# A transformer block on one core: half batch 0's second norm is turned by TensorE in fp32, the filling rows lie on four partitions, and every engine's order is new

## Chip, cores and metric

The kernel runs on one core of a Trainium2 chip. The metric is the device time of one execution in microseconds (us). The profile is of one execution; its span goes from the first instruction to the last.

## The reference

x has 4 batches of 512 rows of 256 numbers, the context 4 x 512 x 512 (256 numbers of keys, 256 of values), the mask 4 x 512.

```python
x = x + tanh(g_xattn[0]) * xattn(ctx, layernorm(x), mask, b)
x = x + tanh(g_ffn[0])   * ffn(layernorm(x), w_gate, w_up, w_down)

# xattn: 8 heads of depth 32
logits  = einsum('bhqd,bhkd->bhqk', Q * depth**-0.5, K) + b[0] - 1e30 * (1 - mask)
out     = einsum('bhqk,bhkd->bhqd', softmax(logits), V)
# ffn: 256 -> 768 -> 256, integer weights times 1/127
h       = silu(x @ wg.T) * (x @ wu.T);  y = h @ wd.T
```

The mask is 1 only at keys at the end of a batch's 512, and every key where it is 0 gets -1e30. So the main path of the kernel takes the last 128 keys alone; a flag computed on the way chooses a general path after it, which these inputs do not take.

## The kernel before

The work is cut into 8 half batches (256 rows each, numbered r = 0 to 7; batch b = r // 2). Every engine has a list of steps written out by hand as short codes in `ORDER` (lines 163 to 205); `step_of` turns a code into a step, and each engine runs its list strictly in order, with waits on semaphores for what other engines make. The codes that matter here:

- `sa`/`sb` statistics of the first/second layer norm (VectorE lines 968 to 977, then GpSimd's power at 658), `na`/`nb` the norm itself in fp32 (VectorE 992 or GpSimd 669, 681), `ha`/`hb` its fp16 high part (ScalarE 745), `la`/`lb` its low part, norm minus high (GpSimd 688), `du` a doubled copy of the query's parts (VectorE 1002).
- `qs` queries turned by TensorE and copied by ScalarE (batch 0), `qn` queries turned by a DMA on SP's queue (batches 1 to 3).
- `kp` the key's high part (VectorE 1048), with its low part on GpSimd (693); `kr` that of batch 0 on VectorE (1040); `ks` keys turned by TensorE and copied out of PSUM by VectorE or ScalarE (1085, 772). From batch 1 on the keys are turned against a matrix `fillers` and not against the identity, so that masked keys are replaced by a mean of the others. `fr` (fill_row, VectorE 1013 to 1017) makes the rows for it from the mask, `ft` (fill_t, TensorE 1284 and 1286, VectorE 1022) the matrix. `br` is the mask row of batch 0 (1007).
- `rm` row maxima of the logits (TensorE 1333, VectorE 1122), `mx` their transpose, `sc` logits and exponential (TensorE 1378 and 1380, ScalarE 821), `ws` weighting of the values and sums (TensorE 1399 and 1404, ScalarE 832 and 834), `at` transpose of the result in fp32 (TensorE 1450), scaling (VectorE 1153 and 1155) and the residual add that makes the new x (GpSimd 698).
- `nn` the second norm turned by a DMA transpose of its high and low parts on SP's queue (582), for halves 0 to 6; `nt` the same by TensorE in fp16, for half 7. `wc`/`wn` cast and DMA transpose of the three weights.
- `hi` six hidden units per half: 8 matmuls (1503), tanh (ScalarE 869), `pr` two VectorE products (1166, 1177), `hs` split of h into fp16 high (ScalarE 878) and low (GpSimd 705), `do` the down projection (TensorE 1529), `fi` finish: residual and store.
- `wu` warm-ups: 3 or 4 matmuls of 512 columns whose result nobody reads (1241), 25 in all; 14 more run at the start.
- `sq`, `ck`, `fs` checks for the flag.

TensorE's results go to eight PSUM banks; the working steps take two of them in turn, and four before the first hidden unit. A step waits until the last user of its bank is emptied (`open_work`). A hidden unit waits for the product of the one two before it.

`norm32` has four slots, and a norm that takes a slot again waits until the low part of the norm that had it is made (`wait_norm_used`).

Of the kernel before, what the change touches and what calls it, by code (L numbers as in the profile page):

```python
# [148 lines left out]
def norm1_on_pool(step):  # L149
# [20 lines left out]
        at2.0 at2.1 sc3.2 hi0.3 ks2.0 hi0.4 rm4.0 ks2.1 hi0.5 do0.0 do0.1 sc3.3 rm4.1 do0.2 rm4.2 hi1.0 hi1.1 do0.3  # L170
        rm4.3 hi1.2 ws3 hi1.3 mx4 hi1.4 at3.0 sc4.0 hi1.5 rm5.0 at3.1 sc4.1 do0.4 do0.5 ks3.0 sc4.2 hi2.0 sc4.3 rm5.1
        hi2.1 ws4 hi2.2 rm5.2 hi2.3 at4.0 ks3.1 do1.0 hi2.4 rm5.3 at4.1 do1.1 do1.2 mx5 do1.3 hi2.5 rm6.0 hi3.0 do1.4
        rm6.1 sc5.0 do1.5 hi3.1 sc5.1 hi3.2 sc5.2 rm7.0 hi3.3 sc5.3 rm6.2 hi3.4 ws5 rm6.3 do2.0 do2.1 at5.0 mx6 hi3.5
        at5.1 do2.2 sc6.0 hi4.0 rm7.1 sc6.1 rm7.2 sc6.2 hi4.1 sc6.3 rm7.3 hi4.2 ws6 mx7 do2.3 hi4.3 do2.4 sc7.0 hi4.4
# [1396 lines left out]
```

## Time and profile before

| what | us |
|---|---|
| median of 3 runs | 137.76 |
| lowest, highest | 137.49, 138.76 |
| profiled execution | 137.66 |
| its span | 135.8 |
| TensorE matmuls busy | 125.0 (92%) |
| VectorE busy | 104.6 (77%) |
| GpSimd busy | 94.0 (69%) |
| ScalarE busy | 91.5 (67%) |

The granted TensorE clock is 0.994 of full speed over the span. The busy share of TensorE counts each matmul to its modelled end, so in a dense stream matmuls overlap and the share is 100%; how far apart they start tells the pace. In the lists PE is TensorE, DVE VectorE, ACT ScalarE, POOL GpSimd, SPq the DMA queue of SP.

### The profile page before, as it was taken

To read this page: it belongs to the slowest core of one execution; us is meant where nothing else is said; L and a number is where in the kernel's file an instruction comes from. 1 tells how busy PE (TensorE), PEld (TensorE's weight loads), DVE (VectorE), ACT (ScalarE), POOL (GpSimd) and SP (SyncE) were. 2 spreads that over 40 slices of the span, in tenths; PEclk is the share of its full clock that TensorE was granted. 3 is DMA by queue.
4 is the path that set the end of the run, shared out by engine and by line. 5 is a ranking of instruction groups with operands and counts; after the bars stand their busy time and mean duration, and the time that the engine had idled before them with its cause. 6 is when DMAs were issued, how large, how long until landed. Compare 5 with 4: busy or idle time off the path is not lost.

```text
span 135.8 us, 3716 instructions
## 1 busy us (share of the span) xinstructions
PE 125.0 (92%) x1276; PEld 97.6 (72%) x1276; DVE 104.6 (77%) x296; ACT 91.5 (67%) x206; POOL 94.0 (69%) x146
## 2 busy tenths in 40 slices
PE   7759799997999997999999999999999999999980
PEld 2245564764868895798799877977986987988860
DVE  1799999999655999599797895796677898678441
ACT  2429997783999867778597896876773644774610
POOL 7464769397999999667956663717866798662920
PEclk9999999999999999999999999999999999999997
DMA  3949999694495404430089702100320080201023
GB/s 127 285 127 369 370 352 155 119 186 89 83 157 116 77 5 76 97 58 7 0 165 234 69 2 57 25 0 0 75 84 0 5 233 1 77 7 47 30 86 92
DMA packets 32050, 14.08 MB, mean 104 GB/s; under 512 B 25605, under 2 KB 31257, under 8 KB 32025
## 3 DMA queue, kind: packets, MB, share of 16 engines
q1 hardware_dynamic: 31984, 13.77, 43.7%
q8 instruction: 12, 0.20, 0.6%
q14 instruction: 14, 0.11, 0.3%
q10 hardware_dynamic: 40, 0.01, 0.0%
HBM read 5.52 MB, written 2.10 MB: 56 GB/s over the span
## 4 chain that ended last, share of the span: by engine, by line
PE 60%; DVE 16%; POOL 9%; DMA 4%; issue 4%; SPq 3%; ACT 2%; DVEq 0%; ACTq 0%; POOLq 0%
PE ps L1503 26%; PE ps L1529 11%; DMA gates<-in_L_xattn_b_dram 4%; PE ps L1399 4%; PE ps L1404 4%; PE ps L1378 4%; PE ps L1380 4%; DVE max_cols L1122 4%; PE ps L1450 3%; PE ps L1333 2%; DVE stats L968 2%; POOL x_sb L698 2%; POOL h L705 2%; DVE gated L1166 2%; POOL q_parts L688 2%
## 5 line engine op out<-in xcount | busy, mean ns | idle before, releaser
L1503 PE MATMUL ps<-n_t,w_gu_t 128*128 128x256 f16 x384 | 49.0, 273 | 0.9 <-DVE h L1177 0.7
L1503 PEld LDWEIGHTS ps<-n_t,w_gu_t 128*128 128x128 f16 x384 | 36.4, 98 | 7.1 <-DVE h L1177 2.1
L705 POOL TENSOR_TENSOR h<-h 128x256 f16<-128x256 f32 x48 | 31.5, 674 | 7.5 <-ACT h L878 7.5
L1166 DVE SCALAR_TENSOR_TENSOR gated<-tanh_h,ps 128x256 f32<-128x256 f32 x48 | 19.9, 415 | 12.3 <-ACT tanh_h L869 11.9
L869 ACT ACTIVATE tanh_h<-ps 128x256 f32<-128x256 f32 x48 | 18.3, 382 | 13.1 <-PE ps L1503 10.9
L1529 PE MATMUL ps<-w_d_t,h 128*128 128x256 f16 x192 | 25.7, 273 | 0.0
L821 ACT ACTIVATE probs<-ps,exp_bias 128x512 f32<-128x512 f32 x32 | 21.6, 686 | 4.3 <-PE ps L1380 4.1
L1122 DVE TENSOR_REDUCE max_cols<-ps 128x4 f16<-128x512 f32 x32 | 21.4, 684 | 2.9 <-PE ps L1333 2.6
L1177 DVE SCALAR_TENSOR_TENSOR h<-ps,gated 128x256 f32<-128x256 f32 x48 | 20.4, 425 | 2.4 <-POOL h L705 0.8
L878 ACT ACTIVATE h<-h 128x256 f16<-128x256 f32 x48 | 18.5, 412 | 4.6 <-DVE h L1177 4.3
L1529 PEld LDWEIGHTS ps<-w_d_t,h 128*128 128x128 f16 x192 | 18.4, 98 | 2.1
L698 POOL TENSOR_TENSOR x_sb<-x_sb,attn 128x256 f32<-128x256 f32 x16 | 11.6, 733 | 8.7 <-DVE attn L1155 8.5
L1378 PE MATMUL ps<-q_stacks,k_stacks 128*128 128x256 f16 x64 | 15.6, 273 | 0.4 <-ACT max_rows L810 0.3
L1380 PE MATMUL ps<-max_rows,kv_rest 128*128 128x256 f16 x64 | 15.5, 273 | 0.0
L968 DVE BATCH_NORM_STATS2 stats<-x_sb 128x6 f32<-128x256 f32 x32 | 11.6, 413 | 4.6 <-DMA x_sb<-in_x_dram 2.5
L658 POOL TENSOR_TENSOR rstd<-var_eps,neg_half 128x2 f32<-128x2 f32 (+1 forms) x13 | 10.5, 806 | 6.7 <-DVE var_eps L977 6.6
L688 POOL TENSOR_TENSOR norm<-norm 128x512 f16<-128x512 f32 x8 | 9.3, 1160 | 6.4 <-ACT norm L745 6.2
L688 POOL TENSOR_TENSOR q_parts<-norm,q_parts 128x512 f16<-128x512 f32 x8 | 9.4, 1180 | 5.8 <-ACT q_parts L745 5.8
L1333 PE MATMUL ps<-k_stacks,q_stacks 128*128 128x128 f16 x128 | 12.1, 219 | 0.0
L1333 PEld LDWEIGHTS ps<-k_stacks,q_stacks 128*128 128x128 f16 x128 | 9.1, 98 | 2.3 <-issue 0.6
L681 POOL TENSOR_SCALAR norm<-x_sb,neg_mean,rstd 128x256 f32<-128x256 f32 x16 | 9.1, 579 | 0.5
L832 ACT ACTIVATE o_sb<-ps 128x512 f32<-128x512 f32 x8 | 4.8, 596 | 6.3 <-PE ps L1404 6.2
(102 smaller groups left out, 180.4 us busy)
## 6 DMA issues: line engine op xcount, KB each, us to landing
x_sb<-in_x_dram SPq DMA_DIRECT2D x8, 256.0 KB, 6.0
out_dram<-x_sb SPq DMA_DIRECT2D x7, 256.0 KB, 2.6
kv<-in_ctx_dram SPq DMA_DIRECT2D x4, 256.0 KB, 6.1
w_raw<-in_L_ffn_w_gate_dram SPq DMA_DIRECT2D x1, 768.0 KB, 7.8
w_raw<-in_L_ffn_w_up_dram SPq DMA_DIRECT2D x1, 768.0 KB, 9.6
w_raw<-in_L_ffn_w_down_dram SPq DMA_DIRECT2D x1, 768.0 KB, 8.4
out_dram<-x_sb SPq DMA_DIRECT2D x2, 128.0 KB, 2.3
q_stacks<-q_parts SPq DMA_TRANSPOSE x12, 3.3
```

Of the source, the lines that this page charges most:

```text
L688: pool.tensor_tensor(low, full, high, ALU.subtract).then_inc(norm_low, 1)
L705: pool.tensor_tensor(h16[:, r % 2, m, 1, :], h32[:, n % NHB, :], h16[:, r % 2, m, 0, :], ALU.subtract).then_inc(h_low, 1)
L821: act.activation(probs[:, j % NPB, :], bank32(SCORES[j % 2]), ACT.Exp, bias=key_bias[:, n:n + 1] if is_wide else exp_bias[:, b:b + 1], sca ...
L878: act.activation(h16[:, r % 2, m, 0, :], h32[:, n % NHB, :], ACT.Copy).then_inc(h_high, 1)
L1122: dve.tensor_reduce(dst, bank32(plan.bank(step)).rearrange("p (h k) -> p h k", h=HG), AX.X, ALU.max, negate=not is_wide).then_inc(emptied_ ...
L1166: mine(dve.scalar_tensor_tensor(out=gated[:, n % 2, :], in0=tanh_h[:, n % 2, :], scalar=1.0, in1=got[:, 0:SH], op0=ALU.add, op1=ALU.mult))
L1177: dve.scalar_tensor_tensor(out=dst, in0=got[:, SH:2 * SH], scalar=0.5 * W_SCALE * W_SCALE * H_SHRINK, in1=gated[:, n % 2, :], op0=ALU.mult ...
L1333: ins = pe.matmul(bank32(n)[:, j * P:(j + 1) * P], q_stacks[:, b, qt, h, :], k_stacks[:, b, h, :], start=(j == 0), stop=(b >= FILL_FROM an ...
L1378: pe.matmul(dst, k_stacks[:, b, h, :], q_stacks[:, b, 2 * half:2 * half + 2, h, :], start=(i == 0), stop=False, skip_group_check=True)
L1380: ins = pe.matmul(dst, (max_sel if is_wide else max_sel16)[:, h, :], (max_rows if is_wide else max_rows16)[:, rows, :], start=False, stop= ...
L1503: ins = pe.matmul(dst, lhs, rhs, start=(w == 0 and (k, l) == terms[0]), stop=(k, l) == terms[-1], skip_group_check=True)
L1529: ins = pe.matmul(dst, lhs, rhs, start=(m == 0 and l == 0 and (t == 0 or r == R - 1)), stop=(m == MT - 1), skip_group_check=True)
```

## The change

Three changes of steps, and new orders for all five engines.

1. Half 0's second norm is no longer split by ScalarE and GpSimd and turned by a DMA (`hb0`, `lb0`, `nn0`). TensorE turns it in fp32 (four transposes) into one PSUM bank; ScalarE copies that to fp16 as the high part; VectorE subtracts this from PSUM for the low part (`nc0`, n_copies).
2. The last mask row of each batch is loaded to a partition of its own, four in all, so that fill_row's three operations are 4x128 in place of 1x384. On TensorE each of three matmuls picks one of the four rows with a selector matrix.
3. The constant tile `ones16` is gone.

```diff
-N_BY_DMA = (0, 1, 2, 3, 4, 5, 6)
+N_BY_DMA = (1, 2, 3, 4, 5, 6)
+N_BY_COPIES = (0,)
...
     "sp": """
-        qn2 wn1 qn3 wn0 nn0 wn2 qn4 nn1 qn5 nn2 nn3 qn6 fi0 qn7 nn4 nn5 fi1 nn6 fi2 fi3 fi4 fi5 fi6 fi7""",
+        qn2 qn3 wn1 wn0 qn4 wn2 qn5 nn1 qn6 qn7 fi0 nn2 fi1 nn3 nn4 fi2 nn5 nn6 fi3 fi4 fi5 fi6 fi7""",
     "pe": """
-        ks0 mt qs0.0 wu5 wu0 qs0.1 rm0.0 rm0.1 wu7 rm0.2 qs1.0 rm0.3 mx0 rm1.0 qs1.1 rm1.1 wu3 sc0.0 sc0.1 rm1.2 sc0.2
-        ft sc0.3 rm1.3 wu6 ws0 ks1.0 mx1 wu2 at0.0 ks1.1 at0.1 sc1.0 rm2.0 rm2.1 wu4 rm2.2 sc1.1 rm2.3 sc1.2 sc1.3
-        rm3.0 rm3.1 mx2 ws1 rm3.2 sc2.0 rm3.3 sc2.1 at1.0 sc2.2 at1.1 mx3 sc2.3 wu1 sc3.0 sc3.1 hi0.0 ws2 hi0.1 hi0.2
...
+        wu0 mt wu6 ks0 qs0.0 wu5 qs0.1 wu1 rm0.0 wu4 ft rm0.1 qs1.0 rm0.2 rm0.3 qs1.1 rm1.0 rm1.1 mx0 wu7 rm1.2 rm1.3
+        sc0.0 sc0.1 wu3 ks2.0 sc0.2 ks1.0 sc0.3 ks1.1 wu2 mx1 ws0 sc1.0 rm2.0 rm2.1 ks2.1 at0.0 sc1.1 ks3.0 rm2.2
+        at0.1 sc1.2 rm2.3 sc1.3 rm3.0 rm3.1 mx2 ws1 sc2.0 rm3.2 sc2.1 rm3.3 at1.0 nc0 sc2.2 rm4.0 mx3 sc2.3 at1.1
+        hi0.0 sc3.0 hi0.1 sc3.1 rm4.1 ws2 sc3.2 rm4.2 hi0.2 rm4.3 hi0.3 do0.0 at2.0 hi0.4 mx4 do0.1 rm5.0 sc3.3 at2.1
+        hi0.5 sc4.0 do0.2 ks3.1 rm5.1 sc4.1 hi1.0 rm5.2 ws3 rm5.3 sc4.2 do0.3 hi1.1 mx5 sc4.3 at3.0 hi1.2 at3.1 sc5.0
+        rm6.0 do0.4 hi1.3 do0.5 rm6.1 sc5.1 hi1.4 ws4 rm6.2 hi1.5 sc5.2 at4.0 do1.0 rm6.3 hi2.0 do1.1 rm7.0 hi2.1 mx6
...
     "dve": """
-        sa0 kp0 br na0 mc kr0 sa1 du0 ks0 mt na1 sa2 rm0.0 du1 eb rm0.1 rm0.2 rm0.3 fr rm1.0 kp1 du2 sa4 rm1.1 rm1.2
-        ft rm1.3 sa6 ks1.0 du3 at0.0 at0.1 rm2.0 rm2.1 rm2.2 sb0 rm2.3 rm3.0 kp2 kp3 rm3.1 du4 rm3.2 rm3.3 at1.0 at1.1
...
+        sa0 kp0 fr na0 kr0 mc sa1 br du0 mt na1 ks0 sa2 rm0.0 du1 kp1 ft rm0.1 eb rm0.2 rm0.3 rm1.0 kp2 rm1.1 rm1.2
+        sa4 du2 rm1.3 ks1.0 kp3 du3 sa6 rm2.0 rm2.1 at0.0 rm2.2 at0.1 rm2.3 du4 sb0 rm3.0 rm3.1 rm3.2 rm3.3 at1.0 nc0
+        rm4.0 at1.1 pr0.0 sb1 ys du5 rm4.1 pr0.1 rm4.2 pr0.2 rm4.3 at2.0 pr0.3 rm5.0 pr0.4 at2.1 pr0.5 rm5.1 rm5.2 du6
+        pr1.0 sb2 rm5.3 pr1.1 at3.0 at3.1 du7 rm6.0 pr1.2 fi0 rm6.1 pr1.3 pr1.4 sb3 rm6.2 at4.0 pr1.5 rm6.3 rm7.0
...
     "act": """
-        ha0 qs0.0 eb ha1 qs0.1 wc0 qs1.0 ha2 wc1 mx0 qs1.1 sc0.0 sc0.1 ha3 sc0.2 sc0.3 wc2 ws0 ha4 mx1 ks1.1 sc1.0 sq0
-        sc1.1 sc1.2 sc1.3 hb0 mx2 ws1 sc2.0 sc2.1 sc2.2 mx3 sc2.3 sq1 ha5 sc3.0 sq2 hi0.0 sc3.1 ws2 hi0.1 ha6 hb1
...
+        ha0 qs0.0 ha1 eb qs0.1 wc0 qs1.0 ha2 qs1.1 mx0 wc1 ha3 sc0.0 sc0.1 ks2.0 sc0.2 sc0.3 ks1.1 mx1 ha4 ws0 sc1.0
+        ks2.1 ha5 sc1.1 ks3.0 sc1.2 sc1.3 wc2 mx2 sq0 ws1 sc2.0 sc2.1 nc0 mx3 sc2.2 hi0.0 sc2.3 hs0.0 sc3.0 hi0.1 sq1
...
     "pool": """
-        sa0 la0 sa1 la1 sa2 na2 la2 na3 la3 sa4 kp1 na4 at0.0 at0.1 sa6 la4 sb0 nb0 lb0 kp2 na5 at1.0 at1.1 na6 la5
...
+        sa0 la0 sa1 la1 sa2 na2 kp1 na3 la2 kp2 la3 sa4 na4 kp3 na5 sa6 la4 at0.0 at0.1 sb0 nb0 at1.0 la5 at1.1 sb1
...
-        mask_row = sb("mask_row", [1, B, P], I32)
+        mask_row = sb("mask_row", [B, P], I32)
...
-        fill_row = sb("fill_row", [P, NF, P], F16)
+        fill_row = sb("fill_row", [P, P], F16)
...
+        def n_copies_out(step):
+            got = bank32(plan.bank(step)).rearrange("p (t k s) -> p t k s", t=2, k=KD)
+            return [n_t16[:, step[1] % 2, :, l * KD:(l + 1) * KD, :] for l in range(2)], got
...
 (ScalarE)
-            act.dma_start(mask_row[:, :, :], mask[:, LAST * P:SK].unsqueeze(0)).then_inc(mask_row_loaded, 16)
+            act.dma_start(mask_row[:, :], mask[:, LAST * P:SK]).then_inc(mask_row_loaded, 16)
...
+                        act.wait_ge(work_filled, plan.filled(step))
+                        parts, full = n_copies_out(step)
+                        act.activation(parts[0], full, ACT.Copy).then_inc(n_high, 1)
...
 (VectorE, fill_row)
-                        mine(dve.tensor_reduce(neg_count[:, :], mask_row[:, FILL_FROM:B, :], AX.X, ALU.add, negate=True))
+                        mine(dve.tensor_reduce(neg_count[:, :], mask_row[:, :], AX.X, ALU.add, negate=True))
                         wait_mine()
                         mine(dve.reciprocal(share[:, :], neg_count[:, :]))
                         wait_mine()
-                        dve.scalar_tensor_tensor(out=fill_row[0:1, :, :], in0=mask_row[:, FILL_FROM:B, :], scalar=1.0,
-                                                 in1=share[:, :].unsqueeze(2).to_broadcast((1, NF, P)),
-                                                 op0=ALU.subtract, op1=ALU.mult).then_inc(fill_row_ready, 1)
+                        dve.tensor_scalar(fill_row[0:B, :], mask_row[:, :], 1.0, share[:, 0:1], ALU.subtract, ALU.mult
+                                          ).then_inc(fill_row_ready, 1)
...
 (VectorE, n_copies)
+                        dve.wait_ge(n_high, plan.nth[step] + 1)
+                        parts, full = n_copies_out(step)
+                        dve.tensor_tensor(parts[1], full, parts[0], ALU.subtract).then_inc(emptied_by["dve"], 1)
...
 (TensorE, fill_t)
-                        pe.matmul(bank32(n)[:, 0:NF * P], ones16[:, :], fill_row[:, :, :], start=False, stop=True,
-                                  skip_group_check=True).then_inc(work_filled, 1)
+                        for i in range(NF):
+                            ins = pe.matmul(bank32(n)[:, i * P:(i + 1) * P], max_sel16[:, FILL_FROM + i, :], fill_row[:, :],
+                                            start=False, stop=(i == NF - 1), skip_group_check=True)
+                        ins.then_inc(work_filled, 1)
...
 (TensorE, n_copies)
+                        pe.wait_ge(normed2, plan.nth["norm2", r] + 1)
+                        for t in range(2):
+                            for k in range(KD):
+                                ins = pe.transpose(bank32(n)[:, (KD * t + k) * P:(KD * t + k + 1) * P],
+                                                   norm32[:, ln_slot("norm2", 2, r), t, k * P:(k + 1) * P], ident32[:, :])
+                        ins.then_inc(work_filled, 1)
...
+                            elif not is_wide and r in N_BY_COPIES:
+                                pe.wait_ge(*plan.emptied(("n_copies", r)))
```

## Rows read from the trace of the kernel before

**Rows 1.** Busy us (instructions) per engine by stretch of the span; then clock, DMA, GB/s.

```profile
...
8.90:38.04 29.14, 26.38 (x279) 18.00 (x280) 26.68 (x81) 23.73 (x41) 21.58 (x26) 1.00 0.83 214
38.04:60.00 21.96, 21.23 (x237) 17.15 (x236) 17.47 (x48) 17.29 (x44) 20.15 (x28) 1.00 0.53 84
60.00:105.00 45.00, 45.00 (x498) 36.88 (x496) 35.65 (x98) 33.37 (x82) 29.07 (x43) 1.00 0.29 54
105.00:120.00 15.00, 14.86 (x141) 12.93 (x139) 11.77 (x34) 8.74 (x24) 11.75 (x18) 1.00 0.26 72
...
```

**Rows 2.** List in time, TensorE: start, us, instruction, [idle before, who ended it].

```profile
...
8.96 0.62 PE L1262 MATMUL ps<-ident,q_parts 128*128 128x128 f16 x8 [0.78 <-DVE q_parts L1002]
...
31.07 0.27 PE L1358 MATMUL ps<-ident,max_cols 128*128 128x128 f16 x2 [0.71 <-DVE max_cols L1122]
...
38.04 1.04 PE L1503 MATMUL ps<-n_t,w_gu_t 128*128 128x256 f16 x8
...
52.64 1.05 PE L1503 MATMUL ps<-n_t,w_gu_t 128*128 128x256 f16 x8 [0.73 <-DVE h L1177]
...
```

**Rows 3.** List in time, GpSimd.

```profile
...
17.20 2.05 POOL L669 TENSOR_SCALAR norm<-x_sb,neg_mean,rstd 128x256 f32<-128x256 f32 x2
...
26.78 1.41 POOL L698 TENSOR_TENSOR x_sb<-x_sb,attn 128x256 f32<-128x256 f32 x2 [2.17 <-DVE attn L1155]
...
31.21 1.50 POOL L681 TENSOR_SCALAR norm<-x_sb,neg_mean,rstd 128x256 f32<-128x256 f32 x2
33.46 1.16 POOL L688 TENSOR_TENSOR norm<-norm 128x512 f16<-128x512 f32 x1 [0.74 <-ACT norm L745]
...
50.36 1.15 POOL L688 TENSOR_TENSOR q_parts<-norm,q_parts 128x512 f16<-128x512 f32 x1
...
```

**Rows 4.** List in time, the DMA issues of SP: issue start, us of the queue.

```profile
...
28.75 1.52 SPq L573 DMA_TRANSPOSE w_gu_t<-w  x1
34.70 1.23 SPq L582 DMA_TRANSPOSE n_t<-norm  x1
...
```

**Rows 5.** DMA issues by tile: count, median us from issue to landing.

```profile
...
n_t<-norm SPq DMA_TRANSPOSE x7, 3.1
w_gu_t<-w SPq DMA_TRANSPOSE x2, 3.8
...
```

**Rows 6.** Chain that ended last, 36 to 44 us: start, us, what.

```profile
...
36.69 0.65 PE ps L1241 x3
...
42.80 0.66 PE ps L1450 x6
...
```

**Rows 7.** List in time, VectorE.

```profile
...
5.11 0.21 DVE L1007 TENSOR_SCALAR bias_row<-mask_row 1x128 bf16<-1x128 int32 x1
5.81 0.74 DVE L992 TENSOR_SCALAR norm<-x_sb,mv,rstd 128x256 f32<-128x256 f32 x2 [0.49 <-POOL rstd L658]
...
12.47 0.68 DVE L1122 TENSOR_REDUCE max_cols<-ps 128x4 f16<-128x512 f32 x1
15.46 0.53 DVE L1013 TENSOR_REDUCE neg_count<-mask_row 1x3 f32<-1x384 int32 x1
...
16.22 1.41 DVE L1017 SCALAR_TENSOR_TENSOR fill_row<-mask_row,share 1x384 f16<-1x384 int32 x1
...
33.57 0.69 DVE L1122 TENSOR_REDUCE max_cols<-ps 128x4 f16<-128x512 f32 x1 [0.27 <-PE ps L1333]
34.65 0.69 DVE L1122 TENSOR_REDUCE max_cols<-ps 128x4 f16<-128x512 f32 x1 [0.38 <-PE ps L1333]
...
50.39 1.40 DVE L1002 COPY q_parts<-q_parts 128x1024 f16<-128x1024 f16 x1
...
```

**Rows 8.** Instructions grouped by line and shape: busy us, mean ns.

```profile
...
L772 ACT ACTIVATE k_stacks<-ps 128x512 f16<-128x512 f32 x5 | 3.0, 597 | 0.1
...
L1085 DVE CAST k_stacks<-ps 128x512 f16<-128x512 f32 x1 | 0.7, 683 | 0.0
...
```

**Rows 9.** Waits of SP's queue: us in total, times, longest.

```profile
...
SPq L581 <- POOL norm L688: 29.0, 4, 9.7
...
```

More of the change, by code:

```diff
@@ L121, in emptied_by_engine @@
 def emptied_by_engine(kind, step):
-    if kind in ("mask_t", "k_stack", "flag_sum", "row_max", "attn_t", "k_block", "fill_t"):
+    if kind in ("mask_t", "k_stack", "flag_sum", "n_copies", "row_max", "attn_t", "k_block", "fill_t"):
         return "act" if kind == "k_stack" and step[1:] in ON_ACT else "dve"
@@ L170 @@
[L170 to L174, printed above, removed]
@@ new lines @@
+    "pool": """
+        sa0 la0 sa1 la1 sa2 na2 kp1 na3 la2 kp2 la3 sa4 na4 kp3 na5 sa6 la4 at0.0 at0.1 sb0 nb0 at1.0 la5 at1.1 sb1
+        hs0.0 nb1 lb1 hs0.1 hs0.2 na6 at2.0 na7 hs0.3 la6 at2.1 sb2 nb2 hs0.4 la7 hs0.5 at3.0 at3.1 lb2 hs1.0 hs1.1
+        sb3 nb3 hs1.2 hs1.3 hs1.4 hs1.5 at4.0 at4.1 lb3 hs2.0 sb4 hs2.1 nb4 at5.0 hs2.2 at5.1 hs2.3 hs2.4 hs2.5 lb4
+        sb5 hs3.0 hs3.1 hs3.2 nb5 hs3.3 hs3.4 hs3.5 hs4.0 lb5 at6.0 at6.1 hs4.1 sb6 nb6 hs4.2 hs4.3 lb6 hs4.4 hs4.5
+        hs5.0 hs5.1 at7.0 at7.1 hs5.2 hs5.3 hs5.4 hs5.5 sb7 nb7 hs6.0 lb7 hs6.1 hs6.2 hs6.3 hs6.4 hs6.5 hs7.0 hs7.1
+        hs7.2 hs7.3 hs7.4 hs7.5""",
@@ L471, in wait_norm_used @@
             if not k.startswith(WIDE):
-                if ("low", w, p) in plan.nth:
+                if ("n_copies", p) in plan.nth and w == 2:
+                    eng.wait_ge(work_filled, plan.filled(("n_copies", p)))
+                elif ("low", w, p) in plan.nth:
                     eng.wait_ge(norm_low, plan.nth["low", w, p] + 1)
@@ L629, in _ @@
             pool.memset(ones_b[:, :], 1.0).then_inc(pool_done, 1)
-            for m in (bias_row[:, :, :], fill_row[:, :, :], ident32[:, :], ident16[:, :], identb[:, :], sum_cols[:, :, :]):
+            for m in (bias_row[:, :, :], fill_row[:, :], ident32[:, :], ident16[:, :], identb[:, :], sum_cols[:, :, :]):
                 pool.memset(m, 0.0).then_inc(pool_done, 1)
@@ L645, in _ @@
                 if part:
-                    pool.wait_ge(pool_done, 15 + part)
+                    pool.wait_ge(pool_done, 14 + part)
                 pool.affine_select(out=head_rows[:, :], in_=head_rows[:, :], compare_op=ALU.not_equal, fill=1.0,
@@ L734, in run @@
                         old = r - (NLB if which == 1 else 2)
-                        if old >= 0:
+                        if old >= 0 and not (which == 2 and old in N_BY_COPIES):
                             if which == 2 and old in N_BY_DMA:
@@ L1003, in run @@
                     elif kind == "bias_row":
-                        dve.wait_ge(pool_done, 11)
+                        dve.wait_ge(pool_done, 10)
                         dve.wait_ge(mask_row_loaded, 16)
-                        dve.tensor_scalar(bias_row[0:1, :, :], mask_row[:, 0:FILL_FROM, :], -SHUT_OUT, SHUT_OUT, ALU.mult, ALU.add
+                        dve.tensor_scalar(bias_row[0:1, :, :], mask_row[0:1, :].unsqueeze(1), -SHUT_OUT, SHUT_OUT, ALU.mult, ALU.add
                                           ).then_inc(bias_row_ready, 1)
                     elif kind == "fill_row":
-                        dve.wait_ge(pool_done, 11)
+                        dve.wait_ge(pool_done, 10)
                         dve.wait_ge(mask_row_loaded, 16)
-                        mine(dve.tensor_reduce(neg_count[:, :], mask_row[:, FILL_FROM:B, :], AX.X, ALU.add, negate=True))
+                        mine(dve.tensor_reduce(neg_count[:, :], mask_row[:, :], AX.X, ALU.add, negate=True))
                         wait_mine()
@@ L1451, in run @@
                         ins.then_inc(work_filled, 1)
+                    elif kind == "n_copies":
+                        r = step[1]
+                        n = open_work(step)
+                        pe.wait_ge(normed2, plan.nth["norm2", r] + 1)
[4 more added lines that the diff above has]
+                        ins.then_inc(work_filled, 1)
                     elif kind == "n_t":
```

53 lines of the change are left out of this document (25 added, 28 removed), and 2 rows, old and new, of the table CODES.

## The prediction, made before the changed kernel had run

> **What bounds the kernel now.** I read the busy time of the engines by stretch first [rows 1]. From 38.04 us, where the first hidden matmuls run, TensorE hardly idles: 0.7 us up to 60, nothing up to 105, 0.1 us up to 120. Before that it has 29.14 us and is busy 26.38. A busy matmul is counted to its modelled end, 0.16 us past the start of a successor (273 ns long, 109 ns apart), so over the seven larger gaps about 3.9 us of the 29.14 are idle. Who ends them stands in the list of matmuls [rows 2]: VectorE's row maxima above all, as at 31.07; the one later gap, 0.73 us at 52.64, waits for VectorE's h. VectorE is the lead-in's second full engine (26.68 of 29.14). So the kernel is a TensorE stream with a fixed tail, and only two things can move its end: TensorE's own work after about 9 us, and its idle time ahead of the stream.
>
> Next the way to the first hidden matmul. GpSimd normalizes at 31.21, ScalarE makes the high part, GpSimd the low part at 33.46, SP issues the transpose at 34.70 [rows 3, 4], it lands 3.1 us later at 37.8 [rows 5], and hidden starts at 38.04. It waits for nothing there, because two groups of scores and one warm-up of three matmuls (0.65 us [rows 6]) stand in front of it.
>
> **Part by part.** Unless said otherwise, times are of the one profiled execution.
>
> Warm-ups: the same 25 matmuls, but wu0 and wu6 (4 and 3) are now ahead of the key stack, in the time before 8.96 us, when TensorE waits for the first doubled query (0.78 us at its end alone [rows 2]). Seven at 0.216 us (three take 0.65 [rows 6]) leave the stretch behind 9: **-1.5 us of TensorE work**. The cover is the wait for half 0's doubled query; it is still there.
>
> fill_row: on one partition its three operations take 15.46 to 17.56, 2.1 us of VectorE between row maxima [rows 7]. On four partitions each handles 128 columns instead of 384. That form is not in the trace; below it is bounded by three 1x128 operations like bias_row's (0.21 each, 0.6 in all), above by the old 2.1. I take 0.65: the row length is what it has in common with bias_row. It moves to 5.15, ahead of norm1 of half 0. The 0.49 us that VectorE waits there for GpSimd's rstd plus bias_row's 0.21 cover it; if mask_row lands late, all of norm1 does. It had landed at 5.11 [rows 7]. fill_t trades one 384-column matmul for three of 128: equal columns, nothing. One memset and the ones tile go from GpSimd's start, off the path.
>
> VectorE's line: from the first row maximum (12.47) to the end of batch 1's last (34.65 + 0.69) are 22.9 us. The new order has the same operations in it except the 2.1 of fill_row, and idle 0.65 (0.27 and 0.38 [rows 7]). Its start comes at 12.75, as bias_row stands in front. 12.75 + 22.9 - 2.1 - 0.65 = **32.9** instead of 35.3.
>
> GpSimd's line: two key low parts, norm1 of half 5 and half 4's low part are pulled ahead of the first residual adds. It fills the 2.17 us that GpSimd waited at 26.78 [rows 3]. The second add still follows its attn_t on VectorE, which comes after two more row maxima and after sa4, sa6, kp3, at about 27.7, so x1 is ready at 28.5; stats 1.2, rstd 0.7, norm2 1.1 give 31.8 for norm2 of half 0, or 32.7 if a pair of norm1 is again held as at 17.20 (2.05 instead of 1.09).
>
> n_copies: removed are the split on ScalarE and GpSimd's 1.16 for the low part [rows 3], and one transpose on SP (1.23 of its queue, 3.1 to land). Added are, first, four fp32 transposes, **+0.44 us** of TensorE (six of this form take 0.66 [rows 6]); one PSUM copy to fp16 on ScalarE, 0.60, and one subtract from PSUM on VectorE, 0.68 at most, the cast's value (rows of the same shapes [rows 8]). The fp32 form is measured, so it carries no range. The Trainium skill, FP8 and Floating Point Precision, TensorE Precision Notes, says that true FP32 takes four passes; the transposes' spacing of 0.11 us against 0.055 for half-precision ones shows two, and by four passes the term would be 0.9 and the sum 0.45 worse. ScalarE's copy holds max_t of half 3 and two exponentials behind it, VectorE's subtract holds rm4.0, at1.1 and the first product. All of these are needed only after the hidden matmul or by it.
>
> TensorE's line: ahead of hidden stood 29.1 - 3.9 = 25.2 us of work. Less 1.5 (warm-ups), less 0.87 (eight matmuls of 109 ns, the scores sc3.0 and sc3.1, that now follow), plus 0.88 (three key stacks and one row maximum, four matmuls of 55 ns each), plus 0.44: 24.1. From 9.0 it could start hidden at 33.1. With the waits: the last row maxima at 32.4, at1.0, n_copies' transposes at 32.7 to 33.1, ScalarE to 34.0 (behind sc2.1's exponential), VectorE to 34.7, hidden at 34.8. I add 0.4 for one VectorE copy held up by GpSimd (below): **35.2 against 38.04**.
>
> SP: weights are turned behind both query turns now. du3 comes near 22.7, so qn3 is through by 26.2 and the two weight turns by 29.2 (1.52 each); w_gu_t lands 3.8 after the issue [rows 4, 5], at 33.0 if I count from the issue's end, before hidden. The down weights and halves 1 to 7 keep their work.
>
> Behind hidden, the work left is what it was: 0.87 added and 0.88 taken cancel, and n_copies' 0.44 is spent already. So the end moves with the start, if no wait is added: -2.8. Of it 1.5 are warm-ups, 1.75 idle time, less 0.44. The profiled execution took 137.66 (span 135.8), the median is 137.76, a tenth away. **137.66 - 2.8 = 134.9.**
>
> **Rivals.** Larger gain: fill_row and the port cost less, and the 0.73 us wait at 52.64 goes too, since its VectorE backlog of row maxima is worked off sooner: 134.9 - 0.7 - 0.7 = 133.5. The bound of all idle time is 3.9 + 0.7 + 1.5 - 0.44 = 5.7, so 132 is the floor.
>
> Port: VectorE's copy at 50.39 took 1.40 instead of 0.42, until GpSimd's subtract of 50.36 was through, and norm1 at 17.20 took 2.05 until the fill was [rows 3, 7]. The new GpSimd line has no idle time from 13 to 28, and six such VectorE operations (kp1 to kp3, du2 to du4) fall into it. Against it: seven of eight such copies took their 0.42. If one and a half more wait 1.0 us, it comes to 136.3, at six to over 139. The Trainium skill, SBUF — State Buffer, Who interferes with whom, says that a two-port VectorE operation and a GpSimd one exclude each other for a whole instruction. By that rule the trace agrees, and it is what speaks against this change.
>
> Given back: VectorE and GpSimd are 80% and 92% busy from 38 to 60 [rows 1]. If TensorE arrives 2.8 us earlier, and product and h_split can't, it waits as at 52.64, several times: 137.3. For it speaks GpSimd's share; against, that low parts for 1.16 and a key part and norms are moved or gone from it.
>
> Slower: the SP queue holds half 2's transpose (nn2) behind qn6, qn7 and finish 0. Before, nn2 stood ahead of those stores and turns. I follow TensorE's order to hidden 2.0 at about 63. du7 comes after at3.1, near 56, finish 0 needs down 0.5, near 58, then 0.74, a store 0.6, and 3.1 to land: 62.4, 0.8 early. From there each us is lost in full. If the doubled query of half 7 or finish is 5.2 us later than this, TensorE stands 4.4 us: 139.3. SP does wait up to 9.7 us for GpSimd's low part in one place [rows 9], so such lateness exists; but a landing that late would need several causes at once.
>
> **How the numbers follow.** Forecast (133.9 to 135.9) 0.54, larger gain 0.10, port 0.16 (half of it still over 1% faster, 0.02 slower), given back 0.11, slower 0.09. About 1%, that is 136.4 and 139.1, is what can be told from no change. Faster: 0.54 + 0.10 + 0.08 = 0.72; same 0.06 + 0.11 = 0.17; slower 0.02 + 0.09 = 0.11. The range leaves out the last 0.09 and some of the floor and of given back: 133.2 to 137.2.
>
> **What would show it.** Right: the fill operations near 5.2 us at about 0.2 each; norm1 of half 0 still at 5.8; the last row maximum of batch 1 done near 33; hidden first at 34.8 to 35.5; n_copies' four transposes in 0.44; idle of TensorE before hidden halved, and next to none after. Wrong: VectorE copies of 1.4 us in 17 to 30 (port); several gaps ended by h in 38 to 60 (given back); hidden 2.0 waiting for a DMA (slower); a norm1 at 6.5 or later (mask_row late).

## The result, and the profile after

| | before | after |
|---|---|---|
| median of 18 executions each, us | 138.69 (137.21 to 140.45) | 137.26 (136.88 to 137.76) |
| ratio of after to before | | 0.9935, 95% interval 0.991 to 0.996 |
| profiled execution, us (span) | 137.66 (135.8) | 137.53 (135.6) |
| first hidden matmul, us | 38.04 | 36.48 |

The change makes the kernel 0.4 to 0.9% faster; 134.9 us was forecast. The two profiled executions differ by 0.13 us alone, because the one of before is among its shorter ones. Among 34 further executions of before, the five with a mean granted clock of TensorE under 0.99 took 138.5 to 141.7 us; none of the 18 of after is under 0.99. Below, gains are read from profiled execution to profiled execution, and ratios are quoted beside them.

Busy time by stretch, the kernel after; the columns are those of [rows 1], the stretches are cut where its own first hidden matmuls run:

```profile
8.90:35.00 26.10, 23.84 (x273) 17.02 (x273) 24.82 (x76) 23.11 (x39) 20.03 (x25) 1.00 0.98 238
35.00:60.00 25.00, 24.21 (x272) 20.30 (x273) 20.71 (x53) 18.96 (x45) 17.98 (x26) 1.00 0.39 75
60.00:105.00 45.00, 43.89 (x473) 35.63 (x471) 32.81 (x91) 30.34 (x80) 29.85 (x44) 1.00 0.29 54
105.00:120.00 15.00, 15.00 (x144) 13.21 (x141) 13.36 (x40) 9.10 (x26) 13.04 (x19) 1.00 0.20 54
```

Up to 60 us TensorE idles as it did, a little less (3.05 us of the span not busy from 8.90, before 3.49); from 60 to 105, where before had it busy all 45.00 us, 1.11 are idle now. Where they are stands in the list in time of TensorE, the kernel after:

```profile
28.29 0.27 PE L1398 MATMUL ps<-max_rows,kv_rest 128*128 128x256 f16 x1
29.50 0.61 PE L1351 MATMUL ps<-k_stacks,q_stacks 128*128 128x128 f16 x8 [0.94 <-issue]
...
33.68 0.60 PE L1477 MATMUL ps<-ident,norm 128*128 128x128 f32 x4
34.12 0.27 PE L1396 MATMUL ps<-q_stacks,k_stacks 128*128 128x256 f16 x1
...
34.45 0.27 PE L1398 MATMUL ps<-max_rows,kv_rest 128*128 128x256 f16 x1
35.38 0.38 PE L1351 MATMUL ps<-k_stacks,q_stacks 128*128 128x128 f16 x4 [0.66 <-DVE attn L1170]
...
36.48 0.71 PE L1533 MATMUL ps<-n_t,w_gu_t 128*128 128x256 f16 x5
...
67.33 0.94 PE L1533 MATMUL ps<-n_t,w_gu_t 128*128 128x256 f16 x7 [1.08 <-DMA n_t<-norm]
```

Three waits count. At 29.50 the row maxima of half 3 start, at 35.38 those of half 4; both read q_stacks, the transposed queries. At 67.33 the hidden matmuls of half 2 start, and a DMA ends their wait. The releaser named at 35.38, VectorE's attn, had ended at 34.87, half a microsecond before: then it was another, and the queue of SP shows which. SP's DMA issues, the kernel after (the second number is the time that the group took the queue, its waits among it):

```profile
21.46 5.47 SPq L598 DMA_TRANSPOSE q_stacks<-q_parts  x4
26.98 4.26 SPq L580 DMA_TRANSPOSE w_gu_t<-w  x2
31.28 3.08 SPq L598 DMA_TRANSPOSE q_stacks<-q_parts  x2
...
52.66 9.23 SPq L598 DMA_TRANSPOSE q_stacks<-q_parts  x4
61.94 1.66 SPq L569 DMA_DIRECT2D out_dram<-x_sb  x1
63.70 1.29 SPq L589 DMA_TRANSPOSE n_t<-norm  x1
```

Eight transposes stand one behind the other from 21.46 to 34.36. Half 4's queries (qn4) are the last of them, behind both weights, and they are issued from 31.28 on, though VectorE had doubled them by 29.87. In the kernel before qn4 had time: rm4.0 came after hidden 0.4. The answer on DMA issues of the stretch 24.5 to 27.5 us gives the median from issue to landing; the kernel after:

```profile
q_stacks<-q_parts SPq DMA_TRANSPOSE x2, 4.9
w_gu_t<-w SPq DMA_TRANSPOSE x1, 4.8
```

In the kernel before, the two query transposes of the same stretch landed in 3.3 us, and the weights in 3.8 [rows 5]. What the DMA engines moved meanwhile, 26 to 31 us in 40 slices, shows where the difference arises:

```profile
GB/s 215 211 197 217 176 191 97 133 197 211 205 156 225 31 0 0 0 0 0 6 8 8 10 8 12 8 166 295 289 269 279 295 291 289 289 295 289 285 295 291
q8 instruction: 1, 0.02, 1.1%
```

From 27.6 to 29.3 us nearly nothing moves, though three transposes are on their way, and just before, at 27.55, one packet of 16 KB runs that the profile lists apart, as "instruction". Row maxima of half 3 start right behind this stop. Such a stop, of 0.6 to 1.5 us and behind such a packet, lies on every query transpose in the traces kept that took 4.9 us or more to land; those that landed in 3.1 to 3.3 us have none over 0.5. In the kernel before the packet came at 32.0, when the queries had landed. No edit moves the packet by itself, so that it causes the stop is not shown; shown is only that the long landings are those under a stop. VectorE, the kernel after:

```profile
5.07 0.27 DVE L1024 TENSOR_REDUCE neg_count<-mask_row 4x1 f32<-4x128 int32 x1
5.37 0.15 DVE L1026 RECIPROCAL share<-neg_count 4x1 f32<-4x1 f32 x1
5.56 0.27 DVE L1028 TENSOR_SCALAR fill_row<-mask_row,share 4x128 f16<-4x128 int32 x1
5.77 0.74 DVE L1003 TENSOR_SCALAR norm<-x_sb,mv,rstd 128x256 f32<-128x256 f32 x2
...
12.70 0.68 DVE L1137 TENSOR_REDUCE max_cols<-ps 128x4 f16<-128x512 f32 x1
...
20.62 0.81 DVE L1013 COPY q_parts<-q_parts 128x1024 f16<-128x1024 f16 x1
...
32.89 1.35 DVE L1137 TENSOR_REDUCE max_cols<-ps 128x4 f16<-128x512 f32 x2 [0.62 <-PE ps L1351]
34.16 0.20 DVE L1168 RECIPROCAL recip<-ps 128x8 f32<-128x8 f32 x1
...
34.95 0.69 DVE L1089 TENSOR_TENSOR n_t<-ps,n_t 128x512 f16<-128x512 f32 x1
```

The operations of fill_row and n_copies took what was forecast. The last row maximum of batch 1 ends at 34.2, not at 32.9, and VectorE waited for TensorE ahead of it.

So hidden 0 comes 1.56 us earlier (2.8 forecast), and of these 1.44 are given back at 60.5 (0.19 us of idle, by the spacing of the matmuls' starts) and at 66.1 (1.25). The rest, old and new gaps against one another, is nothing.

### The profile page after: what moved, and what is told of

Its sections match the earlier page's. It is cut to its first block, busy times and chain, and to the rows that moved or that the text cites. A ratio compares the mean times of both kernels' runs of the same rounds, so it can differ in the third digit from the quotient of the medians.

```text
span 135.6 us, 3725 instructions
## 1 busy us (share of the span) xinstructions
PE 125.1 (92%) x1282; PEld 98.3 (72%) x1282; DVE 105.0 (77%) x297; ACT 90.5 (67%) x206; POOL 92.1 (68%) x144
## 4 chain that ended last, share of the span: by engine, by line
PE 68%; DVE 9%; POOL 5%; issue 5%; DMA 5%; SPq 3%; ACT 1%; DVEq 0%; POOLq 0%
PE ps L1533 28%; PE ps L1559 14%; PE ps L1417 4%; PE ps L1396 4%; PE ps L1398 4%; PE ps L1422 4%; PE ps L1468 3%; PE ps L1351 3%; DMA n_t<-norm 3%; DMA x_sb<-in_x_dram 2%; SPq L598 2%; POOL norm L675 2%; POOL q_parts L694 2%; DVE stats L979 2%; DVE max_cols L1137 1%
## 5 line engine op out<-in xcount | busy, mean ns | idle before, releaser
L711 POOL TENSOR_TENSOR h<-h 128x256 f16<-128x256 f32 x48 | 31.5, 671 | 9.9 <-ACT h L889 9.8
L1559 PE MATMUL ps<-w_d_t,h 128*128 128x256 f16 x192 | 26.5, 273 | 0.1
L889 ACT ACTIVATE h<-h 128x256 f16<-128x256 f32 x48 | 19.1, 414 | 2.7 <-DVE h L1192 2.5
L694 POOL TENSOR_TENSOR norm<-norm 128x512 f16<-128x512 f32 x7 | 8.1, 1160 | 1.3 <-ACT norm L751 1.3
L1417 PE MATMUL ps<-probs,kv 128*32 128x256 f32 x128 | 8.6, 385 | 0.0
```

What stands on the lines that cost most here:

```text
L694: pool.tensor_tensor(low, full, high, ALU.subtract).then_inc(norm_low, 1)
L711: pool.tensor_tensor(h16[:, r % 2, m, 1, :], h32[:, n % NHB, :], h16[:, r % 2, m, 0, :], ALU.subtract).then_inc(h_low, 1)
L889: act.activation(h16[:, r % 2, m, 0, :], h32[:, n % NHB, :], ACT.Copy).then_inc(h_high, 1)
L1559: ins = pe.matmul(dst, lhs, rhs, start=(m == 0 and l == 0 and (t == 0 or r == R - 1)), stop=(m == MT - 1), skip_group_check=True)
```

## Experiments

The theory after the result (**Q**): the transposes queued on SP set when hidden 0 may start, through qn4 and the half-3 queries, and half 2's transposed norm (nn2) on the same queue gives the gain back. Rivals: VectorE's copies, held by GpSimd (**port**); VectorE's and ScalarE's own chain. Each run has executions of before beside it, with medians of 137.6 to 138.3 us, and its ratio is to those; runs of different groups are best compared by their ratios.

**The kernel after again**, nothing edited.

> The changed kernel once more, so that the next three have it beside them on one chip. Queue theory and rivals alike: about 137.3, hidden 0 near 36.5 us, hidden 2 held for the transpose of half 2.

137.17 us, ratio 0.9949 (0.992 to 0.998); hidden 0 at 36.41, hidden 2.0 at 67.23 after 1.23 us of idle. The gaps stand where they did, 0.83 and 1.04 us before rm3.0 and rm4.0 for 1.10 and 0.83.

**nn2 ahead of the store fi0**, in SP's order:

```diff
-qn5 nn1 qn6 qn7 fi0 nn2 fi1 nn3
+qn5 nn1 qn6 qn7 nn2 fi0 fi1 nn3
```

> SP's list with nn2 ahead of fi0. Theory Q (the SP queue holds what TensorE needs): nn2 no longer waits for finish 0 and the blocked store issue (61.94 to 63.60), is issued at about 61.9 right behind qn7, lands at 65.5, before hidden 2's turn at 66.1: the 1.25 us gap goes and the time falls by 1.0 to 1.25. Rival P (products and splits set the pace from 38 us on, so that a gap removed here comes back a few steps later): no change, within 0.3.

136.74 us, ratio 0.9921 (0.988 to 0.996); span 134.5. TensorE at hidden 2.0, and SP's queue, with this order:

```profile
66.45 0.72 PE L1533 MATMUL ps<-n_t,w_gu_t 128*128 128x256 f16 x5 [0.28 <-DMA n_t<-norm]
```

```profile
52.59 10.15 SPq L598 DMA_TRANSPOSE q_stacks<-q_parts  x4
62.85 1.27 SPq L589 DMA_TRANSPOSE n_t<-norm  x1
64.17 0.62 SPq L569 DMA_DIRECT2D out_dram<-x_sb  x1
```

The gap at 66 shrinks from 1.25 to 0.44 us, and the median falls by 0.43 against the kernel after beside it. That the store's place was part of what is given back is shown. Q had the place right and the size too large (1.0 to 1.25): the four query transposes hold the queue for 10.15 us here instead of 9.23, so nn2 goes out at 62.85 and not at 61.9.

**du2 ahead of sa4**, VectorE's copy of half 2's queries put before a group of statistics:

```diff
-        sa4 du2 rm1.3 ks1.0 kp3
+        du2 sa4 rm1.3 ks1.0 kp3
```

> VectorE's list with du2 ahead of sa4 (the place it had in the old order). Theory Q: the query turns of half 2 go out at 19.4 and not at 21.46, the queue is no longer full from 21.5 to 34.4, each transpose lands 3.3 us after its issue and not 4 to 4.9, the gaps of 1.1 us at 28.4 and 0.8 us at 34.5 shrink to under half: hidden 0 starts 0.8 to 1.5 us earlier and the time falls by as much. Rival D (VectorE's line, lengthened by copies held behind GpSimd, is the bound of the lead-in): hidden starts where it did, within 0.3, as VectorE's work is the same.

137.47 us, ratio 0.9978 (0.994 to 1.002); hidden 0 at 36.74. A miss for Q as I had it: the copy began 1.6 us earlier, but took 1.36 us, and du3, which SP needs for the third and fourth query transposes, came 0.9 later (23.80 for 22.88), so the weights were issued at 26.89 for 26.98 and qn4 at 31.71 for 31.28.

**Both moves together.**

> nn2 ahead of fi0 and du2 ahead of sa4 together. Theory Q: the two gains add, 1.8 to 2.7 us, near 135. Rival P: with an earlier lead-in the gaps only come back between 38 and 70 us, and both together give no more than the better one.

136.85 us, ratio 0.9926 (0.989 to 0.996); hidden 0 at 37.60, hidden 2.0 at 67.60. The gains do not add, a second miss for Q; the time is what rival P gave, no more than the better of the two. The profiled execution is the longest of the twelve (137.72), so its hidden 0 is not that of the median. VectorE's copy and GpSimd's list over the same time:

```profile
18.90 2.48 DVE L1013 COPY q_parts<-q_parts 128x1024 f16<-128x1024 f16 x1 [0.20 <-POOL q_parts L694]
```

```profile
18.83 1.16 POOL L699 TENSOR_TENSOR k_parts<-kv,k_parts 128x512 f16<-128x512 f32 x1
19.94 1.16 POOL L694 TENSOR_TENSOR q_parts<-norm,q_parts 128x512 f16<-128x512 f32 x1
```

A copy of 0.42 us waits until two GpSimd subtracts in a row are through, at 21.10, and ends 0.28 after. In the trace of du2 ahead of sa4 alone the same copy took 1.36. The Trainium skill, SBUF — State Buffer, Who interferes with whom, says that whichever of such a pair issues first has the shared ports for its whole instruction; the copy agrees, and it lost to a second instruction as well.

**Both weights first** in SP's order, with nn2 ahead of fi0:

```diff
-qn2 qn3 wn1 wn0 qn4 wn2 qn5 nn1 qn6 qn7 fi0 nn2
+wn0 wn1 qn2 qn3 qn4 wn2 qn5 nn1 qn6 qn7 nn2 fi0
```

> The changed kernel with SP's list beginning wn0 wn1 qn2 qn3 qn4, and nn2 ahead of fi0. Theory Q (the piled-up transpose queue opened the two gaps ahead of hidden 0): the queue was idle until 21.46 with weight 0 cast at 14.2 and weight 1 at 18.7, so both weights are turned before the queries need the queue; qn4 is issued right behind du4 near 29.9 and not at 31.28, lands 3.3 and not 4.0 us later, and the gap of 0.85 to 1.0 us at 34.3 goes, so about 136.0, 0.7 to 1.0 below nn2 first alone (136.74). Rival D (VectorE's and GpSimd's lines bound hidden 0): the gap before the fifth row-maximum group stays or moves behind n_copies, same time as nn2 first. Risk named before: two weight turns among the last input loads can make those land later.

137.06 us, ratio 0.9925 (0.988 to 0.997); hidden 0 at 36.77. The gap before rm4.0 is gone, but wn0, issued at 14.16, holds the queue for 5.70 us and wn1 behind it for 2.90, though ScalarE had cast it at 18.8, and the query transposes begin at 22.86 in place of 21.46; a gap of 1.51 us stands before the matmuls of 26.57. The wait was moved, not won, and Q's 136.0 is missed.

**The four-partition fill alone**, with the orders, the nn0 transpose and the splits of the kernel before.

> The kernel before with the four-partition filling rows alone, in the old orders. Measured by itself, its three operations should take 0.65 us in place of 2.1. Theory L (the lead-in is one chain of row maxima on VectorE): row maxima after them start 1.4 us earlier, hidden 0 up to 1.4 us earlier unless the transpose of half 0's norm holds it, so 0 to -1.0 us in all. Rival: GpSimd's norm1, which the fill held, gains 1 us too, and SP's turns move with it: the full -1.4.

137.76 us, ratio 0.9979 (0.993 to 1.003), unclear by the times. In the profile (136.88, span 135.1) hidden 0 is at 37.32, 0.72 earlier than before, and the wait for h near 51 us is still 0.90. Half of the 1.45 us saved on VectorE reach TensorE.

**n_copies in the orders of before**, together with the four-partition fill; set against the run above, n_copies is what differs.

> The kernel before with n_copies for half 0 alone and the old orders, hidden 0 still behind two groups of the third scores and a warm-up. Theory: the DMA landing was covered by those, so nothing is gained but GpSimd's 1.16 us, and TensorE pays 0.44 us: +0.0 to +0.5. Rival: the landing at 37.8 did hold hidden 0 in the slower executions of the kernel before, then its median falls towards its fastest ones.

137.52 us, ratio 0.9989 (0.994 to 1.004); hidden 0 at 37.48, for 37.32 with the fill alone. Nothing that the times can tell.

**The new orders without n_copies**: half 0's norm is split and turned by SP's DMA again.

```diff
-N_BY_DMA = (1, 2, 3, 4, 5, 6)
-N_BY_COPIES = (0,)
+N_BY_DMA = (0, 1, 2, 3, 4, 5, 6)
+N_BY_COPIES = ()
...
-qn2 qn3 wn1 wn0 qn4 wn2 qn5
+qn2 qn3 wn1 wn0 qn4 nn0 wn2 qn5
```

> The changed kernel with half 0's second norm split and turned by a DMA again (hb0, lb0, nn0), all else in its new place. If the fp32 turn is what lets hidden 0 stand ahead of the third scores, the time rises by 1.5 to 2.5 us (low part 1.16, transpose 3.3 or more in a queue that is already full, less 0.44 of TensorE and 0.7 of copies). If hidden 0 was bounded by the queries' turns anyway: within 0.5.

142.17 us, ratio 1.0268 (1.019 to 1.034): far more than expected. TensorE's list and the busy time by stretch (columns as in [rows 1]; the third from the end is the granted clock):

```profile
39.45 1.89 PE L1533 MATMUL ps<-n_t,w_gu_t 128*128 128x256 f16 x8 [2.79 <-DMA n_t<-norm]
```

```profile
36.00:42.00 6.00, 3.21 (x20) 2.22 (x18) 1.42 (x4) 1.52 (x4) 2.23 (x3) 0.62 0.62 111
42.00:50.00 8.00, 8.00 (x84) 6.01 (x83) 5.36 (x17) 5.10 (x13) 3.58 (x5) 0.86 0.35 68
```

SP's queue is free from 34.47; nn0 is issued at 35.81, when GpSimd has ended the low part (35.72), and lands at 39.4. So it is the split and the landing, not the pile, that hold hidden 0, and it starts 2.97 us later than in the kernel after. TensorE idles 1.49 us before rm4.0 and, after 1.2 us of work, 2.79 us more; then the granted clock is at its lower level, 1.2 GHz (the stretches 39 to 42 and 42 to 44 us read 0.50, from 46 on 1.00): eight hidden matmuls take 1.89 us, elsewhere 1.04. The expected 1.5 to 2.5 us left out this clock, which goes with the rest of the 5 us. n_copies is what makes the new orders possible: 5 us inside them, nothing in the old ones.

**du2 early as a tensor_reduce**: over an axis of length 1, which gives the same values.

```diff
+if r == 2:
+    dve.tensor_reduce(dst, src.unsqueeze(3), AX.X, ALU.max).then_inc(q_doubled, 1)
+else:
     dve.tensor_copy(dst, src).then_inc(q_doubled, 1)
```

> VectorE's copy du2 (q_parts, half 2) stands ahead of sa4 as in the earlier edit, but is written as a tensor_reduce over an axis of length 1 instead of a tensor_copy; all other copies stay. Theory H (a copy of this kind is held while GpSimd's subtracts run, whatever the instruction's length): the reduce has none of the held form and takes 1.0 to 1.3 us by itself wherever it stands, with no stretch to 2.48; it ends by 20.2, the half-2 transposes can be issued on SyncE from about 20.4, and hidden 0 begins at 36.3 to 36.8. Time within 0.3 of the kernel with du2 early. Theory Q (queueing on SyncE alone sets the start, VectorE's copy is nothing): hidden 0 at 36.4 to 36.8 with any length of the copy, the time again 137.0 to 137.5. They part at the instruction: over 1.6 us is against H, under 0.6 shows that the form alone was the price.

137.43 us, ratio 0.9961 (0.993 to 0.999); hidden 0 at 36.61. VectorE:

```profile
18.96 1.22 DVE L1014 TENSOR_REDUCE q_parts<-q_parts 128x1024 f16<-128x1024 f16 x1 [0.20 <-POOL q_parts L694]
```

The instruction is right by theory H: 1.22 us in this trace and in the next, in the same place where the copy took 1.36 and 2.48. For the time H is not the cause: hidden 0 and the median stay.

**The same with nn2 ahead of fi0.**

> The same reduce with SyncE's transposed load nn2 ahead of the store fi0. Theory Q (the load nn2 is late by its place on SyncE, worth 0.4 of the median; nothing else is won by the earlier copy): 136.6 to 137.0, hidden 2.0 at 66.3 to 66.7. Theory H (the held copy ate the gain of the earlier turn): hidden 0 at 35.8 to 36.3, the time 136.1 to 136.5. The first by itself would be the nn2 edit's time again.

136.75 us, ratio 0.9933 (0.990 to 0.996); hidden 0 at 36.53, hidden 2.0 at 66.12. The time of the nn2 edit again, as Q expects.

**Three groups of warm-up matmuls removed** from the kernel after:

```diff
-WARM_UP = (4, 3, 3, 3, 3, 3, 3, 3)
+WARM_UP = (4, 3, 0, 0, 3, 3, 3, 0)
```

> The changed kernel without three of its groups of warm-up matmuls, wu2, wu3 and wu7 (3 matmuls of 128x512 each, about 0.65 us of TensorE each, 1.96 in all; nothing that they write is read). Theory W (the sum on record: what is taken from TensorE's row before hidden 0 is time won until the next wait ends later): row maxima from half 2 on start up to 0.7 earlier, hidden 0 at 35.7 to 36.1, the time 136.5 to 136.9. Theory L (landings of the transposes and the copies of VectorE end TensorE's waits there, so the columns lie in idle time): the gaps grow by about 1.9, hidden 0 at 36.3 to 36.6, the time 137.0 to 137.4. Theory C (the matmuls hold the granted clock): the clock of the stretch up to 40 us falls below 0.97 and the time is 138 or more.

137.17 us, ratio 0.9966 (0.994 to 1.000); clock 0.995; hidden 0 at 36.45. TensorE has 1.96 us less to do and starts hidden 0.03 earlier. In this execution the queries of half 3 landed in 3.3 us, and no gap stands before rm3.0, where 1.10 had been (0.44 stands behind it, ended by VectorE's row maxima). rm4.0 still began at 35.36: qn4 was issued at 30.36, 0.92 earlier than in the kernel after, and landed at 35.27 as before, since the stop of the DMA engines fell on it and on wn0 this time. What they moved from 27.6 to 33 us, in 40 slices:

```profile
GB/s 214 210 150 139 127 197 229 216 214 201 209 207 229 218 218 193 135 174 220 256 233 228 209 334 209 197 199 193 95 9 2 8 8 9 11 9 8 163 288 292
```

Theory L has it. Neither the work of TensorE nor the earlier gap sets the start; the landing of qn4, last in the pile, does.

**The kernel before again**, one more profile.

> The kernel before once more, for a second profile of it beside the one shown. Its executions lie between 137.0 and over 139. Theory V (VectorE's copies held by GpSimd vary from execution to execution): the excess of the eight q_parts copies over 0.42 us each differs by over 0.5 us from the 1.07 of the first profile, and the span with it. Theory S (landings of the transposes vary): the copies repeat within 0.2, and the gaps before row maxima and hidden matmuls differ instead.

137.65 us, span 135.8, hidden 0 at 37.99. The eight copies repeat within 0.02 us each; gaps before 30 us differ by up to 0.5, and make nothing up to hidden 0. Neither theory of the spread was tested, since this execution was no slower than the first.

**One weight fewer.** SP turns only the gate's weights; the up product reads them too, so the hidden values are another function, and the time is read as that of a queue with one transpose less.

```diff
 i = step[1]
+if i == 1:
+    continue
...
-for turned in w_turned[0:2]:
+for turned in w_turned[0:1]:
...
-lhs, rhs = w_gu_t[:, w, m, k, :], n_t16[:, r % 2, :, l * KD + k, :]
+lhs, rhs = w_gu_t[:, 0, m, k, :], n_t16[:, r % 2, :, l * KD + k, :]
```

> The changed kernel without the second transposed load of the gate and up weights (wn1); the up product reads the gate's weights, so the hidden values are another function, with the same instructions on every other engine. Theory Q (the pile of transposes on SyncE sets hidden 0's start): the load wn0 and qn4 land 2.0 to 2.4 us earlier, the gap of 0.82 before row maximum 4.0 closes, the one of 1.10 before 3.0 stays or halves (it stands behind the query turns, ahead of the weights), hidden 0 at 35.5 to 35.8, the time 136.5 to 136.9. Theory V (VectorE's copies and row maxima and ScalarE's own row set it, and the landings only happen to be near): hidden 0 at 36.3 to 36.6 and the time 137.0 to 137.4.

136.36 us, ratio 0.987 (0.980 to 0.994); hidden 0 at 35.44, 1.04 us earlier, no gap before rm4.0. qn4 is issued at 29.93 and lands at 33.8. The stop of the DMA engines lies where it did, from 27.7 to 29.0, so it is not what changed. VectorE's copies are the same as in the kernel after (20.65 0.81, 22.91 0.62, 29.09 0.81), so its chain is not what had held the start.

**The first weight early, in SP's idle time**, nothing left out:

```diff
-qn2 qn3 wn1 wn0 qn4 wn2 qn5 nn1 qn6 qn7 fi0 nn2
+wn0 qn2 qn3 wn1 qn4 wn2 qn5 nn1 qn6 qn7 nn2 fi0
```

> The changed kernel with SyncE's order wn0 qn2 qn3 wn1 qn4 wn2 and so on, and nn2 ahead of fi0: the first weight's transpose is issued alone at 14.2, the second stays between the queries. Theory Q: the pile behind 21.4 is one weight shorter, qn4 is issued near 28.9 to 29.5 and lands by 33.5, the gap before row maximum 4.0 closes, hidden 0 at 35.5 to 35.8; with nn2 in time the median is 135.7 to 136.2, below the 136.74 of the nn2 edit by itself. Theory V: hidden 0 at 36.3 to 36.6 and 136.6 to 136.9. Theory R (the turn at 14.2 meets the loads of x and of the down weight from memory and slows them or is slowed): it takes over 3 us to be issued or lands after 19, and the early row of halves 0 and 1 is later by 0.3 or more; the time 137.0 to 137.5.

**135.54 us** (135.27 to 135.99), ratio **0.983** (0.978 to 0.988), faster than both kernels. SP, then TensorE:

```profile
14.39 5.66 SPq L580 DMA_TRANSPOSE w_gu_t<-w  x1
21.47 5.40 SPq L598 DMA_TRANSPOSE q_stacks<-q_parts  x4
26.91 2.32 SPq L580 DMA_TRANSPOSE w_gu_t<-w  x1
29.92 2.60 SPq L598 DMA_TRANSPOSE q_stacks<-q_parts  x2
```

```profile
34.11 0.39 PE L1351 MATMUL ps<-k_stacks,q_stacks 128*128 128x128 f16 x4
...
35.25 0.94 PE L1533 MATMUL ps<-n_t,w_gu_t 128*128 128x256 f16 x7
...
65.37 1.05 PE L1533 MATMUL ps<-n_t,w_gu_t 128*128 128x256 f16 x8 [0.35 <-DMA n_t<-norm]
```

qn4 is issued at 29.92, as soon as it is doubled, rm4.0 follows without a wait, and hidden 0 starts at 35.25. Right ahead of it n_copies' subtract ends on VectorE, at 35.19 (with one weight fewer at 35.38, for hidden 0 at 35.44), so that chain is the next to hold it. Theory R was half right: beside the loads the early transpose is slow (5.66 us of the queue, 9.8 to land), but it has 7 us until the queries are issued, and all that is lost is 0.2 us before the row maxima of half 2 (25.18 for 24.96). A second queue for the transposes was not tried: the Trainium skill, DMA: Bandwidth & Descriptors, Silent corruption: two transposing streams in flight at once, warns against it, and no run here shows it.

## Why the prediction was wrong

The direction was right, the size was not: 0.13 us between the profiled executions, and 1.4 between the medians, where 2.8 was forecast.

**The steps that held.** fill_row: 0.27, 0.15 and 0.27 us for 0.65, at 5.07, and norm1 of half 0 at 5.77. The first row maximum at 12.70 for 12.75. n_copies: 0.44 us on TensorE (33.68 to 34.12), 0.60 on ScalarE, 0.69 on VectorE for 0.44, 0.60 and 0.68; the sum by four passes is refuted. And "hidden 35.2" is about what the engines allow: with the queue relieved it is 35.25, each link of the chain (n_copies' transposes, ScalarE, VectorE, hidden) 0.45 to 0.6 later than written, which the 0.4 added for one held copy covers; du2, du3 and du4 were held for 0.8 together there.

**Two links were late and cost little.** norm2 of half 0 was ready at 33.05, for 31.8 or 32.7: x1 came at 29.58 and not at 28.5, and no norm was held (1.09 us; the terms from 28.5 on also add up to 31.5). In the relieved run it came 0.2 us ahead of TensorE's own turn at 33.2, so it cost nothing. Batch 1's last row maximum ended at 34.2, with the queue relieved at 33.8, for 32.9, by the held copies and waits for TensorE.

**The step that failed first: SP.** The prediction put "qn3 through by 26.2 and the two weight turns by 29.2", followed the weights to their landing, and stopped. Three things were wrong in it. qn3 was through at 26.93: du2 ended at 21.43, and four transposes in a row follow from there (du3, 23.50 for 22.7, was in time). Two weight turns took 4.26 us of the queue where 1.52 each from [rows 4] made 3.0; the stop of the DMA engines from 27.6 to 29.3 falls on the first, whose issue took 2.71. Where it falls elsewhere, as without three warm-up groups, the two took 3.35, so standing back to back costs little. And qn4, which the new orders put behind the weights and whose rm4.0 they put ahead of hidden 0, had no term at all. Issued at 31.28 it lands at 35.3, and 1.1 us of matmuls follow: 36.48. The experiment with one weight fewer gives 1.04 of the missing 1.28 us back, the early weight 1.23. Of the 1.28, then, the missing term for qn4 is shown by edits; the share of the stop in it (1.6 us, in no term either) is seen in the traces, and no edit takes it away. The landing of half 3's queries, 4.9 us, was hidden behind it: with 3.3 there (the run without three warm-up groups) hidden 0 did not move.

**The step that failed next: what comes after hidden 0.** "The end moves with the start" cost 1.44 us. The rival called slower had the place (nn2 behind qn6, qn7 and fi0) and gave it 0.09 with the landing "0.8 early". Measured: du7 ends at 59.27 (near 56 assumed), the queue is free at 61.9, the store takes 1.66 of it instead of 0.6 (a second stop of the DMA engines, 62.6 to 64.0, falls on it), nn2 is issued at 63.70 and lands at 67.3, where TensorE could have had it at 66.1. The mechanism was that rival's, and its sign, hidden 2.0 waiting for a DMA, appeared. The landing was 4.9 us later than the 62.4 written, near the 5.2 that the rival asked for; its price was 1.25 and not 4.4 because TensorE's own turn, put at about 63, came at 66.1 too.

**Warm-ups, -1.5 us.** The prediction booked more than half of its 2.8 to them, though its 35.2 follows from the chain of waits and not from TensorE's work (33.1). Taking 1.96 us more of them out moved hidden 0 by 0.03: idle time grew by as much. What a stretch loses in work counts only where its end is set by work, and here it was set by a landing. **fill_row** is worth 0.7 by itself up to hidden 0, as the fill alone shows.

**The port rival** had the right observation (VectorE's eight copies took 5.4 us in all, before 4.4) and the wrong weight, and its sign, copies of 1.4 us between 17 and 30, did not appear (0.81 at most): with the hold removed from one of them the time is the same, since SP waited for du3 and then for the pile.

**Given back at h, 38 to 60 us**: the list shows no gap ended by h. One of 0.58 at 54.8, ended by a row maximum, stands where there had been 0.90 for h at 51.7. Not the cause.

Not settled: whether the instruction packet causes the stop of the DMA engines, and what sets its time (27.55 in the kernel after, 30.78 without three warm-up groups); and why the executions of before spread over more than 3 us and those of after over 1.

## What to carry to other kernels

When an order moves transposes on one queue, write down the whole queue for the stretch, each issue with its own service time and what it waits for, and for every consumer which issue it needs: the critical one stood behind those that I had followed. Leave room in it for one stop of over 1 us, which no row of a lone transpose shows. Where the queue has idle time before the pile, one item moved there is worth more (here 1.2 us from one word of an order, 136.74 to 135.54) than the shortening of an engine that feeds it. And of a wait that is shortened, follow the same queue on until the next consumer, with the stores that stand in it.
